# A decoder layer on one core: the feed-forward takes its rows in the order of the experts' token lists

## The reference

```python
x = x + attn(layernorm(x))        # 16 heads, window 128 and 4 sinks
x = x + experts(layernorm(x))     # expert of a token: min(id // 6250, 3)
x = x + ffn(layernorm(x))

# experts, with c = ctx_2048[e], 512 x 512, as all three weights
y = (silu(h @ c.T) * (h @ c.T)) @ c.T
# ffn: rows rounded to 8 bits, weights to three values
h = silu(bit_linear(x, w_gate)) * bit_linear(x, w_up)
h = rms_norm(h, ln_weight)
y = bit_linear(h, w_down)
```

## Time and profile before

| what | us |
|---|---|
| median of 3 runs | 807.55 (807.31 to 810.09) |
| the profiled execution | 806.35 |
| its span, first to last instruction | 804.5 |
| busy: PE, DVE, ACT, POOL | 740.3, 594.6, 473.8, 281.9 |
| steady feed-forward tile, h of one to h of the next | 11.8 |

### The profile page before, as it was taken

How to read it: one execution, slowest core, us unless ns; L and a number is a source line. 1 busy time by engine, 2 the same in 40 slices (tenths; PEclk the granted TensorE clock), 3 DMA queues, 4 the chain that set the end, 5 groups by cost and what they waited for, 6 DMA issues and landing times. The chain is left out here.

```text
span 804.5 us, 14098 instructions
## 1 busy us (share of the span) xinstructions
PE 740.3 (92%) x5150; PEld 507.6 (63%) x5150; DVE 594.6 (74%) x1092; ACT 473.8 (59%) x1025; POOL 281.9 (35%) x282
## 2 busy tenths in 40 slices
PE   5988999999999999999978789999958999999996
PEld 4765777777777777777755568888833433434442
DVE  6885766877668866676576468877638999999975
ACT  5555766666667666766565134444415766776674
POOL 2011204213142131314465144443214564554552
PEclk9998999999999999999999899999989999999999
DMA  9200021114031041302410275554113233433332
GB/s 319 101 1 27 28 72 62 53 33 153 28 106 51 30 147 37 107 27 94 144 53 2 83 280 173 185 198 165 40 58 116 52 83 76 105 92 75 71 79 78
DMA packets 56482, 74.12 MB, mean 92 GB/s; under 512 B 35615, under 2 KB 37663, under 8 KB 54752
## 3 DMA queue, kind: packets, MB, share of 16 engines
q1 hardware_dynamic: 50672, 56.17, 22.8%
q0 software_dynamic: 5456, 16.53, 5.9%
q10 hardware_dynamic: 288, 0.52, 0.2%
HBM read 52.71 MB, written 13.39 MB: 82 GB/s over the span
## 5 line engine op out<-in xcount | busy, mean ns | idle before, releaser
L527 ACT ACTIVATE probs<-s_ps,neg_max 128x512 f32<-128x512 f32 (+2 forms) x256 | 152.5, 611 | 19.0 <-DVE neg_max L696 17.5
L696 DVE TENSOR_REDUCE neg_max<-s_ps 128x2 f32<-128x1024 f32 (+2 forms) x128 | 124.5, 1014 | 35.8 <-PE s_ps L910 35.3
L930 PE MATMUL pT_ps<-ident,probs 128*128 128x128 f32 x832 | 113.9, 277 | 10.4 <-DVE probs L717 9.1
L539 ACT ACTIVATE probs<-pT_ps 128x512 f32<-128x512 f32 x96 | 57.4, 598 | 98.1 <-PE pT_ps L930 97.9
L930 PEld LDWEIGHTS pT_ps<-ident,probs 128*128 128x128 f32 x832 | 92.7, 142 | 25.5 <-DVE probs L717 11.8
L717 DVE COPY probs<-pT_ps 128x512 f32<-128x512 f32 x112 | 76.7, 685 | 36.5 <-PE pT_ps L930 36.0
L1473 POOL TENSOR_TENSOR hw<-h,ln_w_sb 128x512 f32<-128x512 f32 x64 | 83.2, 1311 | 37.3 <-DVE h L1606 35.7
L1717 PE MATMUL gate_ps<-w_tern,xqT 128*128 128x512 bf16 x256 | 66.8, 384 | 13.0 <-DVE h L1606 12.1
L843 PE MATMUL side_ps<-w_hi 128*128 128x512 f32 x172 | 71.0, 413 | 0.0
L1738 PE MATMUL f_y_ps<-w_tern,hqT 128*128 128x512 bf16 x256 | 65.3, 380 | 3.4 <-DMA hqT<-hq 1.8
L843 PE MATMUL side_ps<-w_hi,w_lo 128*128 128x512 f32 x172 | 67.3, 391 | 0.0
(11 more groups left out here) (247 smaller groups left out, 1636.8 us busy)
## 6 DMA issues: line engine op xcount, KB each, us to landing
w_piece<-w_ffn SPq DMA_DIRECT2D x24, 512.0 KB
w_stage<-w_ffn SPq DMA_DIRECT2D x12, 1024.0 KB
xres<-x POOLq DMA_DIRECT2D x4, 1024.0 KB, 5.7
xn<-x SPq DMA_DIRECT2D x12, 256.0 KB, 3.0
xn<-x SPq DMA_DIRECT2D x3, 1024.0 KB
x<-xres POOLq DMA_DIRECT2D x3, 1024.0 KB, 4.8
xn<-c SPq DMA_DIRECT2D x2, 1024.0 KB, 6.1
v_next<-c SPq DMA_DIRECT2D x2, 1024.0 KB, 6.1
```

The source lines that it names most:

```text
L527: nc.scalar.activation(weights[qt][:, h, at:at + width(qt)], s_ps[:, h, 0:width(qt)], ACT.Exp, bias=neg_max[:, qt % 2, h:h + 1], accum_out ...
L539: nc.scalar.activation(out, turned_p, ACT.Identity).then_inc(slot_copied[0], 1)
L696: nc.vector.tensor_reduce(neg_max[:, qt % 2, 2 * s:2 * s + 2], s_ps[:, 2 * s:2 * s + 2, 0:width(qt)], AX.X, ALU.max, negate=True).then_inc ...
L930: last = nc.tensor.transpose(pT_ps[:, k % 2, h * P:h * P + P], weights[qt][:, h, a:z], ident[:])
```

## The change

Beside the list with empty slots there is a dense one: the same order of experts without gaps, 2048 tokens in 16 tiles. The feed-forward takes its row tile t by an indirect gather through dense_rows and its result goes to y by an indirect scatter through the same list. Dense tile t lies within expert tiles 0 to t + 3, so its gather waits for those scatters alone. So the front of tiles 0 to 2 can run in the expert block's last four steps.

- *Attention:* ten more routing operations on VectorE (rows_started, rows_given, rows_addressed), slots_given and slots_addressed in later units than before; sixteen scatters list_dense on GpSimd, four in each group of batch 2; four copies of 1 MB from x to x2 on SP (fill_x2); the load of dense_rows and three waits on SP at the end.
- *Experts:* a class Front holds the front's buffers, semaphores and operations for both blocks; three of its buffers serve as row tiles 8 to 10 before. GpSimd sets the constants early and in steps 11 to 18 gathers feed-forward tiles 0 to 7. Parts of the front stand in steps 15 to 18 on VectorE, GpSimd, ScalarE and TensorE. The sum x2 of the last tile and its scatter move into the next block; there is no wait for the scatters at the end.
- *Feed-forward:* the loads, constants, table load, 20 products and the fronts of tiles 0 and 1 are gone from its start; ln_w is still loaded there. Stores and gathers of tiles 8 to 15 are GpSimd's. hw takes the buffer xg_own.

```diff
-KEPT_BUSY = {"experts": 10, "ffn": 20}
-ROUTE_COUNTED, ROUTE_STEPS = 10, 32
+KEPT_BUSY = {"experts": 10}
+ROUTE_COUNTED, ROUTE_STEPS, ROUTE_DENSE = 10, 34, 42
...
+                def fill_x2(b):
+                    sp.dma_start(x2[b * SEQ:b * SEQ + SEQ, :], xin[b * SEQ:b * SEQ + SEQ, :]).then_inc(x2_filled, 16)
...
                         load_piece(b, 7)
+                        fill_x2(b)
                         if b + 2 < BATCH:
                             load_piece(b + 1, 0)
...
                 sp.dma_start(rows[:], slot_tokens.rearrange("(p s) one -> p (s one)", p=P)).then_inc(list_loaded, 16)
+                fill_x2(BATCH - 1)
                 batch(BATCH - 1, True)
+                sp.wait_ge(dense_written, 16 * IDS)
+                sp.dma_start(sh["dense_rows"][:], dense_tokens.rearrange("(p s) one -> p (s one)", p=P)).then_inc(dense_loaded, 16)
...
+                def list_dense(b, g):
+                    n = IDS // HG
+                    pool.wait_ge(route, ROUTE_DENSE)
+                    for t in range(n * (g - 1), n * g):
+                        nc.gpsimd.indirect_dma_start(dense_tokens, bass.IndirectOffsetOnAxis(dense_at[:, t:t + 1], 0),
+                                                     token_no[:, t:t + 1], None).then_inc(dense_written, 16)
...
                             list_tokens(b, g)
+                        if b == BATCH - 2:
+                            list_dense(b, g)
...
-                for qt, route_part in enumerate((tiles_needed, slots_given, slots_addressed, experts_of_tiles)):
+                for qt, route_parts in enumerate(((tiles_needed, rows_started), (slots_given,), (), (slots_addressed, experts_of_tiles))):
...
+                            if (b, g, qt) == (0, 1, 2):
+                                rows_given()
+                            if (b, g, qt) == (0, 1, 3):
+                                rows_addressed()
...
+    def gather(self, pool, t):
+        homes = len(self.homes)
+        for s in range(0 if t == 0 else t + EXPERTS - 1, t + EXPERTS):
+            self.wait_scattered(pool, s)
+        if t >= homes:
+            pool.wait_ge(self.y_stored[t % homes], (t - homes) // homes * 16 + 16)
+        self.nc.gpsimd.indirect_dma_start(self.home(t), None, self.x2, bass.IndirectOffsetOnAxis(self.sh["dense_rows"][:, t:t + 1], 0))\
+            .then_inc(self.x_loaded[t % homes], 16)
...
+                front.set_consts(pool)
+                last = ROUTED_TILES - 1
                 for s in range(ROUTED_TILES):
...
+                    if s == last - 2:
+                        front.rstd_of(pool, 0)
+                        front.rstd_of(pool, 1)
...
+                    if 0 <= s - X_LATE < len(front.homes):
+                        front.gather(pool, s - X_LATE)
+                    if s == last - 1:
+                        pool.wait_ge(mean_ready, 1)
+                        front.gu_scale_of(pool, 0)
+                        front.rstd_of(pool, 2)
-                scatter(ROUTED_TILES - 1)
-                pool.wait_ge(scattered, 16 * ROUTED_TILES)
+                front.gu_scale_of(pool, 1)
...
+                    if s == ROUTED_TILES - 3:
+                        front.wait_scattered(act, 8)
+                        front.normalize_x(act, 0)
+                    if s == ROUTED_TILES - 2:
+                        front.normalize_x(act, 1)
+                front.wait_scattered(act, 10)
+                act.wait_ge(front.consts, 4)
+                front.xqT_of(act, 0)
...
+                    if s == last:
+                        front.top_of_x(dve, 1)
+                        front.scale_x(dve, 1)
                     if inside(s - 1):
                         x2_of(s - 1)
...
+                    if s == last - 3:
+                        front.stats_of(dve, 0)
+                        front.variance_of(dve, 0)
+                        front.stats_of(dve, 1)
+                        front.variance_of(dve, 1)
+                    if s == last - 2:
+                        front.mean_of(dve, 0)
+                        front.mean_of(dve, 1)
+                    if s == last - 1:
+                        front.top_of_x(dve, 0)
+                        front.scale_x(dve, 0)
+                        front.wait_scattered(dve, 9)
+                        front.quantize_x(dve, 0)
                     if chunk_of(s) is not None:
                         clip(chunk_of(s))
-                x2_of(ROUTED_TILES - 1)
+                    if s == last - 1:
+                        front.stats_of(dve, 2)
+                        front.variance_of(dve, 2)
+                front.quantize_x(dve, 1)
                 dve.wait_ge(w_ready, CHUNKS)
...
+                pe.wait_ge(front.consts, 4)
+                front.transpose_x(pe, 0)
                 y_of(ROUTED_TILES - 1)
+                front.transpose_x(pe, 1)
...
+                def store(t):
+                    pool.wait_ge(y_ready, t + 1)
+                    nc.gpsimd.indirect_dma_start(y, bass.IndirectOffsetOnAxis(sh["dense_rows"][:, t:t + 1], 0), xt[t], None)\
+                        .then_inc(y_stored[t % len(homes)], 16)
...
+                pool.wait_ge(front.x2_ready, ROUTED_TILES)
+                front.wait_scattered(pool, last_expert - ROW_SEMS)
+                nc.gpsimd.indirect_dma_start(x2, bass.IndirectOffsetOnAxis(sh["rows"][:, last_expert:ROUTED_TILES], 0), xg[last_expert], None,
+                                             bounds_check=last_row, oob_is_err=False).then_inc(front.scattered[last_expert % ROW_SEMS], 16)
                 pool.wait_ge(lnw_loaded, 16)
...
                     weighted(t, 3)
                     if inside(t + 2):
-                        gu_scale_of(t + 2)
+                        front.gu_scale_of(pool, t + 2)
+                    if inside(t - LATE_DOWN):
+                        store(t - LATE_DOWN)
+                    if t >= LATE_DOWN + 1 and inside(t - LATE_DOWN - 1 + len(homes)):
+                        front.gather(pool, t - LATE_DOWN - 1 + len(homes))
                 rms_of(TILES - 1)
+                for t in range(TILES - LATE_DOWN, TILES):
+                    store(t)
...
-                for n in range(KEPT_BUSY["ffn"]):
-                    nc.tensor.matmul(y_ps[:], ident[:], gate_w[:, 0, 0:D], start=True, stop=True)
-                transpose_x(0)
```

More of the change, by code:

```diff
@@ L1043, in expert_phase, with expert_rows @@
+def expert_rows(sh, front):
+    return front.homes + front.expert_homes + [sh["xg_own"][:, s, :] for s in range(OWN_TILES)]
+def expert_phase(nc, io, x1, x2, sh, front):
     with ExitStack() as ctx:
@@ L1063, in expert_phase @@
         e_ones = sb("e_ones", [P, P])
[L1065 to L1066 removed]
+        xg = expert_rows(sh, front)
         assert len(xg) == ROUTED_TILES
@@ L1484, in _ @@
                         rms_of(t - 1)
+                    if t < 2:
+                        for s in range(ROUTED_TILES - OWN_TILES + t * FC, ROUTED_TILES - OWN_TILES + t * FC + FC):
+                            front.wait_scattered(pool, s)
                     weighted(t, 0)
@@ L1700, in _ @@
             def _(pe):
-                pe.wait_ge(consts, 4)
-                def transpose_x(t):
-                    pe.wait_ge(xq_ready, t + 1)
-                    for k in range(DK):
-                        last = nc.tensor.transpose(xT_ps[:, k, :], xq_code[:, k * P:k * P + P], ident[:])
-                    last.then_inc(xq_transposed, 1)
                 def gate_up(t, c):
@@ L1747, in _ @@
                         gate_up(t, c)
-                        if c == 1 and inside(t + 1):
-                            transpose_x(t + 1)
+                        if c == 1 and t and inside(t + 1):
+                            front.transpose_x(pe, t + 1)
                         if inside(t - LATE_DOWN):
```

330 lines of the change are left out of this document (182 added, 148 removed).

## The result

The changed kernel takes 803.0 us (median of 12 runs, 800.3 to 804.5), the kernel before 807.7 us (12 runs, 804.0 to 810.1): a ratio of 0.9948, with a 95% interval of 0.9931 to 0.9965. That is 4.7 us or 0.5% less, at the border of what can be told from no change. The forecast was 802.15 us. The profiled run took 803.17 us with a span of 801.3.

What follows compares the result with a forecast made beforehand. TensorE bounds attention and experts, VectorE the steady feed-forward, with a hole between experts and feed-forward. Terms +3.3 + 0.7 - 0.4 - 10.5 + 0 + 1.5 = -5.4 us gave 802.15 us, range 797 to 809.

Steps and rivals of the forecast that it cites:

- Part 1: Attention: four list scatters before the batch boundary make TensorE wait, +3.3 us; low clock after it +0.7; first units -0.4.
- Rival B: Attention: x1 store's wait shrinks when issued later, so TensorE is not stopped; total -9.4, 798.2 us; chance 0.11.
- The first units' -0.4: Early attention: routing instructions moved out of the unit where TensorE waits 3.02 us for VectorE; -0.4 us net.
- Part 2: Last expert tiles: front work on VectorE delays the last product by 1.45 us.
- Part 3: Experts to feed-forward: first gate product 12.1 us sooner, partly lost waiting for ln_w; -10.5 us together with part 2.
- I take 1.2 us, since no landing is waited for: Phase change: the block's barrier, the only thing left there, was put at 1.2 us.
- Rival A: Phase change: the 4.7 us barrier is mostly GpSimd's closing and block change; total -1.9, 805.7 us; chance 0.19.
- ln_w holds h of tile 1: First feed-forward tile: ln_w's load takes 6.1 us, landing after the first h; h of tile 1 comes at 609.2.
- rival D: Something else than ln_w holds the first tile, or expert order costs another 2 us; about 804 us; chance 0.09.
- Part 4: Steady feed-forward tiles: GpSimd's scatter and gather, 2.5 to 3.1 us, fit into 3.5 us of room; 0 us.
- rival C: Feed-forward: scatter and gather exceed 3.5 us, GpSimd sets the pace; +9.6, 811.8 us; chance 0.11.
- Part 5: End: the last store, an indirect one from GpSimd, is issued and lands later; +1.5 us (+0.9 to +3.4).

Runs made afterwards that it cites:

- list ahead: Changed kernel with the sixteen dense-list scatters issued after groups 1 to 3 of batch 2 (6, 5, 5), none after group 4: ratio 0.9907, 799.3 us.
- plain store: Changed kernel with the last row tile stored by a plain DMA from SyncE, GpSimd waiting for it: ratio 0.9936 to the kernel before.
- old order: Changed kernel with the first attention units' routing steps back in their old places: ratio 0.9973 to the kernel before.
- the weights' addresses: Changed kernel with dense_rows' home taken behind the shared tensors, so routed weights keep the earlier kernel's addresses: ratio 0.9944 to the kernel before.
- GpSimd quiet: Changed kernel with no GpSimd DMA in the last expert tile: gathers one tile earlier, tile 17's scatter behind the phase change. Ratio 0.9899, 798.7 us.
- chain behind the change: Changed kernel with statistics, rounding and transposes of tiles 0 to 2 back behind the phase change, after 12 keep-busy products; gathers stay early. Ratio 0.9979.
- GpSimd quiet and the new order: Changed kernel with list ahead, GpSimd quiet, SyncE waiting for last scatters, and late VectorE and GpSimd front work moved back: ratio 0.9829, 793.1 us.
- plain store and SyncE waiting: Changed kernel with the last row tile stored by a plain SyncE DMA that SyncE, not GpSimd, waits for: ratio 0.9901 to the kernel before.

## Why the prediction held, and where it did not

**Part 1** was right in place, cause and nearly in size: +4.0 forecast, +4.3 in the trace, of which the wait is 3.4 for the forecast's 3.3. With the list away from the boundary 3.3 us came back by the ratios. Rival B (the list hidden) is out. The x1 store's wait shrank from 4.98 to 4.30 us, the 0.7 us that spoke for rival B and that the forecast had allowed. The first units' -0.4 is -0.55 by the first mark, but that agreement is luck: the same mark lies anywhere from 384.65 to 388.62 in the twelve traces with the new order, for 387.12 before. Only the shorter wait of TensorE, 0.84 us, is shown.

**Part 2** was right: 10.11 us from act_sb of tile 17 to the last product became 11.34, +1.2 for the +1.45, and moving VectorE's instructions away brings 10.25.

**Part 3** came out near its sum by two errors of size that cancel, and one thing it left out.
- "I take 1.2 us, since no landing is waited for" failed. It was 3.1 us behind TensorE's last transpose, since GpSimd's last instruction, and not a landing, sets the release, about 4 us later. Rival A named the cause ("GpSimd's own closing and the block change"), and 1.9 us of its 3.5 came true.
- That ln_w holds h of tile 1 was right in its mechanism, and its term was too large. In all eight traces whose clock is 1.00 behind the release, h of tile 1 comes 6.98 to 7.00 us behind GpSimd's first product with ln_w (the forecast had 7.15; its four products and one rstd add up to 607.8 and not to 608.0), while from the first gate product it is 11.57 to 11.88 us. What was off is the load: it landed 4.5 to 4.8 us behind its issue, not 6.1. This gave 1.4 to 1.7 us back. The kernel before has nearly the same distance from the first gate product (608.08 to 619.71), but there GpSimd's first product waits for h and not for ln_w, so the likeness is chance.
- The clock was left out. The profiled run of the changed kernel shows exactly the 13.25 us from the first gate product to h of tile 1, and for another reason: half clock from 600 to 605 us, with h 8.8 us and not 7.0 behind the first product with ln_w. It would have passed for a confirmation. In this run, then, something else than ln_w held the first tile, as rival D has it. Four traces with the same phase change and full clock behind it (list ahead, plain store with either waiter, old order) give -10.3 to -10.6 us for parts 2 and 3, where the forecast had -10.5; the one with low clock to 604 us (the weights' addresses) gives -10.0, the two with half clock to 605 give -8.6 and -8.7.

How ln_w reaches h shows in VectorE's instructions of that first tile. VectorE has no idle time from 603.23 to h of tile 1, and its rounding of a row tile, 0.49 us with nothing beside it (at 606.33 in the kernel before), takes 1.50 us while GpSimd multiplies by ln_w (the run with GpSimd quiet):

```profile
602.61 3.91 POOL L1669 TENSOR_TENSOR xg_own<-h,ln_w_sb 128x512 f32<-128x512 f32 x3 [1.52 <-DMA ln_w_sb<-ln_w]
603.23 0.75 DVE L1758 SCALAR_TENSOR_TENSOR h<-up_ps,gu_scale,f_gate 128x512 f32<-128x512 f32 x1 [0.96 <-PE up_ps L1849]
603.89 1.50 DVE L1211 TENSOR_SCALAR xq_big<-f_xn,x_inv 128x512 f32<-128x512 f32 x1
605.32 0.68 DVE L1179 BATCH_NORM_STATS2 f_bn_st<-xn 128x6 f32<-128x512 f32 x1
...
606.33 0.75 DVE L1758 SCALAR_TENSOR_TENSOR h<-up_ps,gu_scale,f_gate 128x512 f32<-128x512 f32 x1
...
607.17 2.52 DVE L1764 TENSOR_REDUCE hw_max<-xg_own 128x1 f32<-128x1024 f32 x2
...
609.61 0.74 DVE L1758 SCALAR_TENSOR_TENSOR h<-up_ps,gu_scale,f_gate 128x512 f32<-128x512 f32 x1
```

The second of GpSimd's three products, in a timeline of GpSimd around 604 alone:

```profile
603.84 1.27 POOL L1669 TENSOR_TENSOR xg_own<-h,ln_w_sb 128x512 f32<-128x512 f32 x1
```

It ends at 605.11 and the rounding at 605.39. In all eight traces the rounding ends 0.27 to 0.29 us behind the end of that product, whether it began 1.24 or 1.55 us before. So a later ln_w makes VectorE's whole chain later by as much. The Trainium skill (SBUF — State Buffer, "SBUF: two separate sides") says that GpSimd and a VectorE instruction in a two-port mode lock each other out of a shared pair of ports for a whole instruction; the rounding that ends only behind GpSimd's product is what that rule would give, and the trace agrees.

**Part 4** was right to 0.1 us: 11.80 us a tile in all fourteen traces of this case, so rival C is out. The gathers in the feed-forward fit into the hole.

**Part 5** was mis-sized: +1.5 forecast, +3.0 measured, inside its upper bound of 3.4. The runs split it: 1.0 for the issue, 2.1 for GpSimd being the engine that waits last. The forecast's term was a later landing. That was paid only to 0.9 us: the last scatter landed 2.7 us behind its issue, not 3.5, and the last plain store 2.0. Which engine waits was not in the forecast.

**Not forecast:** -1.4 us in the expert tiles, where three steady ones take 19.14 us instead of 19.42. Its cause was not found. Four of the other traces (chain behind the change, plain store, GpSimd quiet, GpSimd quiet and the new order) have the same faster tiles and yet 123.1 to 124.2 us in this stretch, as much as the kernel before or more, with low clock between 468 and 477 us.

With a low-clock stretch less at the change of phase (2.0 us) the terms of the profiled run would sum to -5.2, against -5.4 forecast and -4.7 by the medians. The total was right, but the meeting (+1.9), the load of ln_w (-1.4 to -1.7), the end (+1.5) and the expert tiles (-1.4) were each off: that it agrees to 0.9 us is partly luck.

## What to carry to other kernels

Work that is taken off the path at a change of phase pays only as far as the slowest engine lets the block close: look at each engine's last instruction there, and let GpSimd finish early, with small work moved behind the change. An added queue of DMA issues belongs where nothing behind it on that engine is needed soon: the same sixteen scatters in earlier groups took 3.4 us of TensorE's wait away. And before a distance in one trace is taken for a confirmation, look at the granted clock in it, and measure it from the mark that it is said to hang on: of two distances to h of tile 1, only the one from ln_w's first product stayed the same from trace to trace.

## What was not expected of the hardware

- GpSimd's last instruction to the release of the next block: 4.16 to 4.39 us in eight traces, 3.92 us with no DMA on it for 12 us; hidden when it ends 4.8 us or more ahead of the release, as in the three traces where TensorE's end came later. TensorE's last transpose to the release: 0.3 us. A second, empty meeting: 0.65 us. What GpSimd does in those 4 us no row shows.
- At the end of the program: 4.3 us from the last scatter's issue if GpSimd waits for it, 3.1 us if SyncE does; 4.6 and 2.5 us from the last sum with a plain store. The last scatter lands 2.7 us behind the start of its issue, the plain store 2.0 us.
- VectorE's rounding of a 128x512 row tile beside GpSimd's products with ln_w: 1.24 to 1.55 us instead of 0.49, always ending 0.27 to 0.29 us behind the end of the product beside it; GpSimd's next product then takes 1.45 us instead of 1.26.
- Low clock after a stop of TensorE does not come each time. Behind the same stop at the change of phase (3.1 us from TensorE's last transpose to the release in both) the stretch from 600 to 605 us ran at 0.50 in the changed kernel (its row stands above) and at 1.00 in the run with the plain store and SyncE waiting, whose busy times by stretch have this row:

```profile
600.00:605.00 5.00, 4.86 (x23) 2.28 (x24) 3.17 (x7) 3.00 (x5) 1.28 (x2) 1.00 0.57 210
```
